# A graph layer with gathered and counted edges: 19 rounds that gather 4 and 5 units by turns instead of 18 rounds of 5, rows found one round ahead, unit columns turned one step sooner, first transfers in order of use

## The reference

```python
h = x @ node_w.T
rf = edge_attr_64 @ review_w.T
m = (h[src] + rf) * edge_weight1
agg = jax.ops.segment_sum(m, dst, num_segments=12500)
y = x + agg
out = (y - mean(y, -1)) / sqrt(var(y, -1) + 1e-5)
```

## Time and profile before

| | before |
|---|---|
| median of 3 runs | 2188.84 us (2188.12 to 2189.43) |
| the profiled execution | 2191.23 us, its span 2189.4 us |
| busy | DVE 85%, PE 84%, POOL 72%, ACT 65% of the span |
| mean granted TensorE clock | 0.924 of full speed |
| chain that ended last | POOL 63%, issue 20%, PE 7%, DVE 6% |
| DMA | 173.28 MB, 79 GB/s on the mean |

### The profile page before, as it was taken

One profiled execution on the slowest core, in us unless ns is written; L12 is line 12 of the kernel. 1 busy time (PEld: TensorE's weight loads), 2 busy tenths in 40 slices (PEclk: granted clock), 3 DMA queues, 4 the chain that ended last, 5 costly groups with the idle time before them and its releaser, 6 DMA issues.

```text
span 2189.4 us, 95528 instructions
## 1 busy us (share of the span) xinstructions
PE 1842.9 (84%) x35999; PEld 1621.5 (74%) x36000; DVE 1854.2 (85%) x5664; ACT 1432.4 (65%) x2705; POOL 1582.9 (72%) x1539
## 2 busy tenths in 40 slices
PE   1669798979898989888898899889988997989984
PEld 1558687868787878777787788778877886878874
DVE  3859797979798989888898899789978897979974
ACT  1547675767676766766676667566766775767744
POOL 3777777777777777777777777777777777777501
PEclk8679898989999999989999999899989998989997
DMA  7223333333343333333333334333433343333302
GB/s 144 50 64 84 82 83 75 85 75 84 81 88 80 87 80 88 80 85 73 87 83 84 72 86 86 81 74 84 88 76 73 83 92 75 81 76 86 69 4 59
DMA packets 480122, 173.28 MB, mean 79 GB/s; under 512 B 443549, under 2 KB 455397, under 8 KB 479445
## 3 DMA queue, kind: packets, MB, share of 16 engines
q1 hardware_dynamic: 426791, 111.57, 23.8%
q0 software_dynamic: 49632, 51.95, 10.7%
q10 hardware_dynamic: 3218, 3.20, 0.7%
HBM read 163.39 MB, written 3.20 MB: 76 GB/s over the span
## 4 chain that ended last, share of the span: by engine, by line
POOL 63%; issue 20%; PE 7%; DVE 6%; DMA 2%; ACT 1%; DVEq 0%; POOLq 0%; ACTq 0%; SPq 0%
POOL rows L541 60%; PE x_ps L1493 3%; PE count_ps L1480 3%; POOL work L567 2%; DVE hot_lo L865 2%; DVE hot_key L864 1%; DMA counts<-dst 1%; POOL dst_row L559 1%; PE unit_ps L1405 1%; DMA dst_row<-dst,row_i 1%; ACT x_tab L1361 1%; DVE work L1000 0%; ACT counts L1283 0%; DVE x_tab L1020 0%; DVE x_tab L1008 0%
## 5 line engine op out<-in xcount | busy, mean ns | idle before, releaser
L541 POOL DMA_INDIRECT rows<-x,g_src_cols x1440 | 1496.1, 1039 | 443.4 <-issue 438.4
L1283 ACT ACTIVATE counts<-count_ps 128x588 f32<-128x588 f32 (+1 forms) x1192 | 836.0, 746 | 617.5 <-PE count_ps L1480 615.0
L1480 PE MATMUL count_ps<-hot_key,hot_lo 128*128 128x294 f32 x4552 | 863.5, 325 | 242.3 <-DVE hot_lo L865 177.4
L865 DVE SCALAR_TENSOR_TENSOR hot_lo<-count,cols 128x256 fp32r<-128x256 f16 x2276 | 1051.8, 477 | 1.0
L1480 PEld LDWEIGHTS count_ps<-hot_key,hot_lo 128*128 128x128 f32 x4552 | 664.2, 195 | 347.3 <-issue 170.5
L1493 PE MATMUL x_ps<-counts,x_tab 128*64 128x63 f32 x21364 | 789.7, 227 | 19.4 <-DVE sums L779 18.4
L1493 PEld LDWEIGHTS x_ps<-counts,x_tab 128*64 128x64 f32 x21364 | 715.7, 140 | 77.0 <-issue 26.1
L864 DVE TENSOR_SCALAR hot_key<-count,cols 128x294 fp32r<-128x294 f16 x1734 | 668.0, 385 | 71.7 <-PE count_ps L1480 60.1
L1240 ACT ACTIVATE hot_key<-far_key,all_ones 128x294 fp32r<-128x294 f16 x542 | 293.6, 542 | 17.6
L1238 ACT ACTIVATE far_key<-count,neg_key 128x294 f16<-128x294 f16 x542 | 284.7, 525 | 0.1
L1405 PE MATMUL unit_ps<-rows,g_hot 128*32 128x64 f32 x5760 | 120.1, 245 | 0.0
(11 more groups left out here) (199 smaller groups left out, 768.5 us busy)
## 6 DMA issues: line engine op xcount, KB each, us to landing
rows<-edge_attr SPq DMA_DIRECT2D x196, 512.0 KB
rows<-x,g_src_cols POOLq DMA_INDIRECT x1440
out<-x_tab SPq DMA_DIRECT2D x12, 256.0 KB
counts<-dst SPq DMA_DIRECT2D x1, 848.0 KB
a_stage<-dst SPq DMA_DIRECT2D x17, 48.0 KB
a_stage_w<-edge_weight SPq DMA_DIRECT2D x17, 48.0 KB
g_stage<-src SPq DMA_DIRECT2D x18, 40.0 KB
g_stage<-dst SPq DMA_DIRECT2D x18, 40.0 KB
```

Source lines behind the costliest of these rows:

```text
L541: pool.indirect_dma_start(out=g_x[:, i, t, :], out_offset=None, in_=x, in_offset=bass.IndirectOffsetOnAxis(ap=g_src_cols[at.p][:, k:k + 1] ...
L865: dve.scalar_tensor_tensor(hot_lo[h][:, :, :], count16[:, 0:P].unsqueeze(1).to_broadcast([P, 2, P]), cols_[:, LO, j:j + 1], cols_[:, W_LOW ...
L1283: act.activation(to, count_ps[(g + e) % 2][:, 0:n, 0:KEYS].rearrange("p a (h d) -> p a h d", d=D), ACT.Copy).then_inc(counts_read, 1)
L1480: done = pe.matmul(count_ps[(g + e) % 2][:, k % 2, 0:KEYS], hot_lo[h][:, i, :], hot_key[h][:, :], start=(i == 0), stop=(i == 1))
```

## The change

The change gives 19 rounds. Even rounds have 4 gathered units and odd ones 5 (`G_OF`), 85 in all, where there were 90; the last round has 5 groups instead of 6. So there are 113 groups where there were 108, and 111 a units where there were 106. The hardware loop still has 8 iterations of two rounds; three rounds are written out behind it instead of two.

- `compare` and `find_rows` work two rounds ahead, in step 1 instead of step 0, and `find_rows` stands right behind `find_runs`; `gather_row` of the round after next stands behind `gather_runs` of the next.
- `prepare_g`, `turn_g` and `take_src` stand in step 0 instead of step 1, and `load_g_stage` works two rounds ahead.
- In the head, `a_dst` and `u_dst` are each loaded by two transfers (96 and 15 rows, 80 and 5 rows), `u_dst` and the weights behind `a_dst`, and features and node table only once the first runs have landed; the table goes over SP's queue instead of ACT's. `sums` is set to zero early, a third by DVE and two thirds by ACT. The checks stand behind `prepare(0)`, and the mean of the weights before the flag.
- In the last round the preparation of the spills stands in step 2 instead of 3.

The diff, cut to its core:

```diff
-ROUNDS = 18
-GATHERED = 5
+ROUNDS = 19
+LAST_RG = 5
+G_OF = (4, 5)
+GATHERED = max(G_OF)
...
             def load_g_attr(at, i):
 
-                u, s = at.r * GATHERED + i, (at.p * GATHERED + i) % ATTR_BUFS
+                u, n = units_before(at) + i, in_pair(at, i)
+                s = n % ATTR_BUFS
                 if not isinstance(u, int) or u >= ATTR_BUFS:
-                    sp.wait_ge(g_summed, u - ATTR_BUFS + 1 + GATHERED)
+
+                    sp.wait_ge(g_summed, u - (1 if n == 0 else 3 if n == 1 else 2) + 1 + GATHERED)
...
-            load_g_stage(0)
-            sp.dma_start(a_dst, dst[A_FROM:EDGES].rearrange("(u t e) -> u t e", t=UT, e=P)).then_inc(a_dst_loaded, 16)
+            load_g_stage(BEGIN)
+            for u0, u1 in ((0, A_UNITS // 16 * 16), (A_UNITS // 16 * 16, A_UNITS)):
+                sp.dma_start(a_dst[u0:u1, :, :], dst[A_FROM + u0 * UNIT:A_FROM + u1 * UNIT].rearrange(
+                    "(u t e) -> u t e", t=UT, e=P)).then_inc(a_dst_loaded, 16)
+            sp.wait_ge(a_dst_loaded, 32)
             load_a_stage(0)
...
+            sp.wait_ge(runs_landed, 48)
+            sp.wait_ge(consts_ready, 1)
             for i in range(ATTR_BUFS):
-                load_g_attr(Round(0, 0), i)
-                load_a_attr(Round(0, 0), i)
+                load_g_attr(BEGIN, i)
+                load_a_attr(BEGIN, i)
+                if i == 0:
+                    sp.dma_start(x_tab[:, 0:BY_P, :], x[0:BY_P * P, :].rearrange("(h l) f -> l h f", l=P)
+                                 ).then_inc(x_tab_loaded, 16)
...
                 if not isinstance(at.r, int) or at.r >= 1:
-                    pool.wait_ge(g_summed, at.r * GATHERED + i + 1)
+
+                    ago = G_OF[1 - at.p] if i < min(G_OF) else sum(G_OF)
+                    pool.wait_ge(g_summed, units_before(at) + (i - ago + 1 + GATHERED))
...
-                    gather_row(ahead.r)
                     gather_unit(ahead, 0)
                     gather_runs(ahead.r)
-                    for i in range(1, GATHERED):
+                    if not is_near_end(at):
+                        gather_row(ahead.r + 1)
+                    for i in range(1, units(ahead)):
                         gather_unit(ahead, i)
...
-            prepare(0)
-            dve.memset(sums[:, :], 0.0).then_inc(added, BEGUN_ADDS)
-
+
+            dve.wait_ge(w_turned, 1)
...
-                    if g == 1 and not last:
+                    if g == 0 and not last:
                         prepare_g(at.r + 1)
...
-                        if k == 12 and g == 0 and not last:
-                            find_rows(at.r + 1)
                         if k == 14:
-                            if g == 1 and not last:
+                            if g == 0 and not last:
                                 take_src(at.r + 1, 1 - at.p)
...
                         if k == 22 and g == 1 and not last:
+                            if not is_near_end(at):
+
+                                dve.wait_ge(compared_all, at.r + 3)
                             find_runs(at.r + 1)
+                            if not is_near_end(at):
+                                find_rows(at.r + 2)
...
-                        if e == 2 and g == 0 and not last:
-                            compare(at.r + 1)
+                        if e == 2 and g == 1 and not is_near_end(at):
+                            compare(at.r + 2)
```

More of the change, by code:

```diff
@@ L374, in is_ok, with after, groups, units @@
             return eng.value_load(ok_tab[0:1, 0:1], min_val=0, max_val=1)
-        Round = namedtuple("Round", "r p")
+        Round = namedtuple("Round", "r p h")
+        BEGIN, LAST = Round(0, 0, 0), Round(ROUNDS - 1, (ROUNDS - 1) % 2, (ROUNDS - 1) // 2)
+        def after(at):
+            return Round(at.r + 1, 1 - at.p, at.h + at.p)
+        def groups(at):
+            return LAST_RG if is_last(at) else RG
+        def units(at):
+            return G_OF[at.p]
+        def in_pair(at, i):
+            return at.p * G_OF[0] + i
+        def units_before(at):
+            return at.h * sum(G_OF) + at.p * G_OF[0]
         def first(at, g):
@@ L495, in load_round, with unit_after @@
+            def unit_after(at, g):
+                n, of_pair = in_pair(at, g), sum(G_OF)
+                if n + ATTR_BUFS >= of_pair:
+                    return after(at), of_pair - 1 - n
+                later = g + ATTR_BUFS
+                return (at, later) if later < units(at) else (after(at), later - units(at))
             def load_round(at):
-                for g in range(RG):
+                for g in range(groups(at)):
+                    if g == 2 and not is_near_end(at):
+                        load_g_stage(after(after(at)))
@@ L624, in _ @@
             gather_runs(0)
+            gather_row(1)
             gather_tiles(begun, 0, range(3 * UT // 4, UT))
-            for i in range(1, GATHERED):
+            for i in range(1, units(begun)):
                 gather_unit(begun, i)
@@ L1051, in _ @@
             take_src(0, 0)
-            dve.wait_ge(a_dst_loaded, 16)
+            dve.memset(sums[:, 0:ZEROED], 0.0).then_inc(added, 1)
+            dve.wait_ge(a_dst_loaded, 32)
             dve.tensor_tensor(a_diag, ident[0:A_UNITS, 0:A_UNITS].unsqueeze(1).to_broadcast([A_UNITS, UT, A_UNITS]),
@@ L1172, in step_of @@
                             make_hot(at, c, k)
-                        elif k >= GW and not (last and c == RG):
+                        elif k >= GW and not (last and c == LAST_RG):
                             make_hot(at, c + 1, k - GW)
@@ L1287, in _ @@
             read_g(0, 0)
+            act.activation(sums[:, ZEROED:NODES + WIN], eps[:, 0:1].to_broadcast([P, NODES + WIN - ZEROED]), ACT.Copy,
+                           scale=0.0).then_inc(added, BEGUN_ADDS - 1)
             act.wait_ge(samples_spread, 1)
@@ L1319, in step_of @@
                             read_counts(at, c, e)
-                            if not (last and c == RG):
+                            if not (last and c == LAST_RG):
                                 keys_after(at, c, e)
@@ L1550, in step_of @@
                     for k in range(GW):
-                        if k == SUM_G and g < GATHERED:
+                        if k == SUM_G and g < units(at):
                             sum_g(at, g)
                         if k == TURN:
-                            if g == 1 and not last:
+                            if g == 0 and not last:
                                 turn_g(at.r + 1)
```

200 lines of the change are left out of this document (104 added, 96 removed).

## The result

The changed kernel takes 2093.77 us (median of 3 runs, 2090.01 to 2097.24). The ratio to the kernel before is 0.956, with a 95% interval of 0.9534 to 0.9586. The forecast was 2093.0. The profiled execution took 2093.77 us, its span is 2091.6 us.

What follows compares the result with a forecast made beforehand. The prediction took POOL's gathers to pace the kernel, through DVE's wait for the row of `dst`. Its sum was 2189.4 - 128 - 27 + 85.5 - 7 - 5 - 23 + 9 = 2094, forecast 2093 us, range 2068 to 2128.

Steps and rivals of the forecast that it cites:

- (a): DVE's run search: its wait for POOL's row of `dst` goes, the row being asked for a round earlier; -128 us.
- (b): Steps behind the row wait: PE's catching up goes with it, -27 us, leaving 210.0 us per pair of rounds.
- (c): Round count: one round more without a loop head, the last round losing one group; +85.5 us.
- (d): Gathered units: 85 instead of 95 with one round more, 0.7 us saved for each; -7 us.
- (e): Instructions moved between steps: free in the sum, except that DVE's wait for the comparison in step 0 goes; -5 us.
- (f): Head: split load and early zeroing bring the first matrix at 48.2 instead of 72.88 us; -23 us, bounds -10 and -30.
- (g): Start of step 4 of round 1: DVE waits once for round 2's runs, landing at 245.5 against 236.8; +9 us.
- (h): Feature buffers shared by a pair's last and the next pair's first unit: 33 us cover a 2.4 us load; nothing.
- Who paces: Pair of rounds in the loop: compute paces with 208.7 us against POOL's 204.7, a margin of 2%.
- the POOL case: POOL's gathers get dearer and still pace; break-even 1.373 us, rows suggest 1.356; at 1.42, 2150 us; chance 0.10.
- The hidden things: A feature or stage load, or the loop's return elsewhere in the code, comes out: 14 us, 2107 or 2079; chance 0.14.
- TensorE's clock: PE holds the low clock of 0.86 in all 112 steps: +207 us, 2300, slower than before; chance 0.03.

Runs made afterwards that it cites:

- rows_late: Changed kernel with the comparison, row search and fetch of rows put back to their old places: 2111.4 us, ratio 0.9657 to the kernel before.
- five_each: Changed kernel with 18 rounds of 5 gathered units and 6 groups each, early rows and new head kept: 2174.9 us, ratio 0.9948.
- one_load: Changed kernel with `a_dst` loaded by one transfer of 111 rows instead of two of 96 and 15: 2097.3 us, ratio 0.9588.
- zero_late: Changed kernel with `sums` set to zero by DVE alone, in one memset ahead of the flag as before the change: 2090.2 us, ratio 0.955.
- fewer_gathers: Changed kernel with units 0 to 3 of every round from 1 on fetching 14 of 16 blocks, so output lacks source rows: 2079.2 us, ratio 0.9501.
- four_rounds: Changed kernel with four rounds per loop iteration instead of two, three returns instead of seven: 2101.0 us, ratio 0.9618.
- runs_four: Changed kernel with comparison and searches in step 0, runs and row fetched ahead of all units, and four rounds per loop iteration: 2094.2 us, ratio 0.9589.

## Why the prediction was right, step by step

- **(a), (b), the row wait and the catching up.** Right in place, and the pair takes 208.75 us, forecast 208.7. `rows_late` and `five_each` say why. The prediction gave the gain to the row being asked for earlier. Early rows alone would have moved the wait to `prepare`; it's the smaller share of gathers in a round that ends it. The sum had both, so its number stood.
- **(b), its size.** Its own terms, 8 x 15.8 + 21, are 147.4 us and not "some 155", so the term should have read -19 and not -27. And the pair that it took for all was a short one. The kernel before has, for round 0 and for the sixteen rounds behind it:

```profile
109.44:233.14 123.70, 98.36 (x1996) 86.74 (x1988) 99.00 (x305) 78.01 (x147) 95.67 (x92) 0.90 0.35 77
233.14:2046.65 1813.51, 1599.19 (x31682) 1408.02 (x31674) 1587.96 (x4891) 1242.40 (x2319) 1403.14 (x1347) 0.94 0.37 81
```

Against 8 x 210.0 - 7.9 = 1672.1 (the last pair has no return) that is 141.4 us, and round 0 shrinks by 22.6 more, to the 101.1 that it takes with the change: 164 in all, and so -36 for (b). The slip in the sum hid half of that error.
- **(c), (d), (e), groups and units.** Outside the head, the eight pairs and the tail the sum leaves 268.4 us, and 266.6 came. In it the new wait is 6 us too small, so the rest was some 8 us too large, about what (b) lacked.
- **Luck.** The terms were off by up to 9 us in both directions and the total by less than 1 us; that they cancelled is luck. Without the slip in (b) the forecast would have been 2101.
- **(f), the head.** First matrix 48.2 forecast, 47.3 measured; first sums 86.4 and 84.6. The split transfer took 5.8 us, and `one_load` puts 5.7 us of the first sums on it. But "the head: -23" doesn't stand as a term by itself: `zero_late` gives 8.5 us of it back and costs nothing measurable.
- **(g), the new wait.** Right in its place, forecast at 236.8 with 9 us, measured 14.7. DVE arrived at 236.2, and the runs landed at 250.9 instead of 245.5. The first row was asked for at 25.3 instead of 24.5, and the rest of the delay is dearer gathers. More important, (f) and (g) are one term: what POOL needs from the first row to the runs of round 2 sets the time there, and of the head only what brings that row sooner counts.
- **(h), feature buffers.** Nothing, as forecast: PE's sums held DVE's `g_hot` for 7.4 us in 7 times, before 7.1.
- **Who paces.** The verdict held, the margin didn't: 1.368 us for a gather, above the bound of 1.356, and 0.4% instead of 2% (0.7% by the pairs in the loop). One sign that was named didn't come: POOL was to have waits of its own in later rounds, and has none, which the prediction had listed among the signs of the POOL case. The margin was too thin for it; the waits of 113.3 us come only in `fewer_gathers`, where the pair stays as it is, and that decides for compute. The thin margin cost nothing here, and it's one reason why `four_rounds` and `runs_four` missed.
- **The rivals.** POOL doesn't pace, but the reason given against it was wrong in part (below). The hidden things stayed hidden; the seven returns cost 7.3 us each beyond an ordinary step, not 7.9. The mean granted clock rose from 0.924 to 0.961, so TensorE's clock didn't stay low.

## What to carry to other kernels

Where an engine waits once a round for one that works ahead, count both sides' time for a round: if the one ahead has more to do, an earlier request only moves the wait to the next hand-over, and if it has less, the late request costs little (some 20 us here, most of it in the first rounds, where the waits had been 134). Once two or three sides are within 1% of each other, a gain on one is given back on another (four returns were worth 27 us with POOL relieved and nothing without), so price a further change against the second limit. A saving in the head counts only up to the first place where the engine that works ahead is waited for; ask which engine's start sets that place.

## What the runs showed that was not expected

**POOL's slow gathers end with DVE's instructions.** The prediction said that the trace before shows none of the blocking between GpSimd and VectorE. That was misread. Among POOL's indirect DMAs of 0.94 to 1.35 us there are 29 of over 2 us behind 50 us, of which this one stands at the start of step 1 of round 0, with DVE beside it (kernel before):

```profile
110.39 0.22 DVE L693 TENSOR_SCALAR g_first_at<-first_mask,g_first 80x10 f32<-80x10 f32 x1
...
110.53 3.12 POOL L541 DMA_INDIRECT rows<-x,g_src_cols  x1 [0.30 <-issue]
...
112.57 0.26 DVE L722 TENSOR_TENSOR g_hot<-column,g_cols 128x112 f32<-128x112 f32 x1
```

It ends at 113.65, 0.82 us after the end of that `g_hot`. All 29 before, and 27 of the 29 over 1.9 us in the changed kernel, end 0.81 to 0.83 us after the end of such an instruction, and 28 of the 29 there begin in the stretch behind `prepare_g` or `prepare_a`, in which DVE goes from instruction to instruction without a pause until it ends with that `g_hot`. Not all that begin there are held: 30 others before take 0.94 to 1.11 us. The mean of the long ones is 2.86 us with the change and 2.43 before: 25 of them now meet the matrices of three windows, where 9 did and 20 met two. From 110 to 1900 us the long ones exceed 1 us by 48.8 us in all, before by 38.4. That is 0.008 us for each of the 1315 and 1328 DMAs of that stretch, of the 0.014 by which their mean rose (1.057 from 1.043); the others rose too (1.020 from 1.014).

In the head it is plainer still. In the changed kernel:

```profile
9.92 5.27 POOL L598 DMA_INDIRECT rows<-x,g_src_cols  x1 [0.31 <-issue]
15.49 2.61 POOL L598 DMA_INDIRECT rows<-x,g_src_cols  x1 [0.30 <-issue]
```

They end 0.83 and 0.82 us after L1116 and L1123, two instructions of 1.95 and 2.28 us with two operands from SBUF. The first began at 9.92, 2.5 us ahead of L1116, when DVE was in the memset that L1116 follows without a pause. In `zero_late` those two stand elsewhere, and POOL's gathers go with them:

```profile
10.04 1.84 POOL L598 DMA_INDIRECT rows<-x,g_src_cols  x1 [0.31 <-issue]
12.19 3.16 POOL L598 DMA_INDIRECT rows<-x,g_src_cols  x1 [0.30 <-issue]
```

The two instructions begin at 9.04 and 12.25 there, and the gathers end again 0.83 and 0.82 us behind their ends. In `one_load` the first of the two comes at 17.87, where it meets half a microsecond of POOL's eighth gather and does it no harm, and all but the first of those eight take 0.94 to 0.96 us, even beside the memset of 3.53 us, which has a pause of 5.3 us behind it there. The Trainium skill, page "SBUF — State Buffer", section "Who interferes with whom", says that GpSimd and a VectorE instruction in a 2-port mode want the same pair of ports, and that the later one fully blocks for the whole instruction of the other. The trace agrees that POOL is held, not that one instruction is the measure: the long ones wait through four to eight of them, while other gathers pass beside the same kinds of instruction in 1.02 us. That ports are what holds them is not shown by any run; nor was it tried whether a pause behind `prepare_g` would free POOL.

**An engine needn't be full to have no room.** ACT was busy 72%, and a sixth key of 21 cost over 20 us (0.9682 against 0.956), and most of that in one step of six.
